# First attention of a two-layer network: TensorE's order of work, the tail's softmax by tile, and the output bias

## The chip, the cores and the metric

The kernel is one launch on one core of one Trainium2 chip. The metric is the device time of the launch in microseconds (us). The kernel before took 3280.93 us in the median of three runs (3278.07 to 3284.38). The engines are TensorE (PE; its weight loads are PEld), VectorE (DVE), ScalarE (ACT), GpSimd (POOL) and SyncE (SP), which issues DMAs. Everything is float32 unless stated.

## The reference, cut to what matters

```python
# x is (8, 512, 256); a layer is half a feed-forward, an attention, half a feed-forward
x = x + 0.5 * L0_ffn(layernorm(x));  x = x + L0_attn(layernorm(x));  x = x + 0.5 * L0_ffn(layernorm(x))
x = x + 0.5 * L1_ffn(layernorm(x));  x = x + L1_attn(layernorm(x));  x = x + 0.5 * L1_ffn(layernorm(x))
# L0_attn: 16 heads of 16, a window of 32 earlier tokens
disp, val = x @ w_disp + b_disp, x @ w_val + b_val
strain = disp_window - disp                              # (B, head, T, 32, 16)
state = mean over the window of (strain @ w_state + b_state)
bond = gelu(strain @ w_strain + b_strain + state @ w_state_i + state_window @ w_state_j + rel_pos @ w_pos)
damage = sigmoid(gelu(strain @ w_damage + b_damage) @ w_damage_out + b_damage_out)
logits = bond @ w_bond_out + b_bond_out - 10 * damage    # masked where the window starts before token 0
out = (softmax(logits) over the window, applied to val_window) @ w_cproj + b_cproj
```

## The kernel before, in words

The network is six phases in a row: feed-forward, first attention, feed-forward, and the same three for the second layer. Only the first attention (`attn0_phase`, L1650 on) is touched. Every engine runs a list of instructions in the order in which it is written and waits on semaphores.

**Chunks and steps.** A batch of 512 tokens is 16 chunks: two halves of eight heads, each with eight groups of four window places. The phase is a loop over steps s (`for s in range(LAST)`, written once for each engine); batch i is s // 16 and the step within it is q = s % 16. There are 128 chunks and 29 steps behind them. For chunk n, DVE makes the bond input in four operations (`bond_chunk`, L2316), POOL the damage input in one (`damage_chunk`, L1984), ACT puts a Gelu over each (L2247, L2252), and TensorE contracts both with a 32-column weight (`columns`, L2031, eight instructions each). Both inputs have rings of three buffers: chunk n is written once TensorE has summed chunk n-3. In step s, DVE and POOL make chunk s+1, ACT handles chunk s, and TensorE sums chunk s-1.

**In the same steps.** Every four chunks ACT makes a tanh (L2260), DVE combines (L2327), TensorE transposes the logits (L2039), and DVE copies them out. At steps 3, 5 and 7 of a batch the softmax of the batch before runs: maximum on DVE (L2350), subtraction on POOL (L1991), exponential on ACT (L2266), sums on DVE (L2355). The softmax rows go to DRAM in 128-byte pieces and come back skewed (`skew_weights`: four stores, L1898, and one load of 2 MB, L1903). Each of the 32 tiles of 128 tokens is then finished in four steps, a new tile every four steps (`finishing`): transposes of the weights (`turn_weights`, L2054), copies by ACT and DVE, 32 small products with the values (`sums`, L2065), division (L2373), transposes (L2092), a copy (L2392), projection with the bias as a one-row product (`project`, L2099, L2100), and addition to x (L2398). A tile's transposes wait for the addition of the tile before.

**Products of a batch.** TensorE makes the terms q, a and c of both halves (`make_q` L2127/L2130, `make_a` L2137/L2140, `make_c` L2147), the values (L2084), the transposed tokens (L2108) and their window means (L2115, L2118), at the steps `A1_Q`, `V_Q`, `XN_Q` and so on. In TensorE's step they all stand ahead of `columns(s - 1)`, which is last. DVE copies each of them out in the same step, behind its own tile work. POOL normalises the tokens of the next batch at step 5 (L1973), and those of batch 0 ahead of the loop.

## Time and profile before

| | |
|---|---|
| median of three runs | 3280.93 us |
| the profiled execution | 3305.36 us |
| its span | 3303.6 us |
| start of the phase to its first chunk on ACT | 670.4 to 720.03 us |
| its 128 chunks | 720.03 to 1364 us |
| its tail, to the last addition | 1364 to 1455.4 us |

The span is cut by the profile's own clock, from the first instruction. The phase begins when the engines leave the barrier at 670.4 us. The row of a stretch gives each engine's busy time; a timeline row gives a start, a length and, in brackets, how long the engine had been idle and who released it. The mean granted TensorE clock of the whole execution was 0.929 of full speed.

### The profile page before, as it was taken

How to read it: one execution, taken by the hardware profiler on the slowest of the kernel's cores; microseconds unless marked ns; L12 is line 12 of the kernel's file. 1: busy time of each engine (PE TensorE's matmuls, PEld its weight loads, DVE VectorE, ACT ScalarE, POOL GpSimd, SP SyncE). 2: the span in 40 equal slices, each digit the busy share in tenths (PEclk: the TensorE clock that was granted, in tenths of full speed). 3: DMA queues.
4: the chain of work that ended last, by engine and by line, in shares of the span. 5: the costliest groups of instructions: out<-in, count | busy, mean ns of one | idle time of the engine just before them, and what ended most of it. 6: DMA issues, size and time to landing. Idle time of an engine off the chain costs nothing. (4 is left out here: it accounts for less than half of the span.)

```text
span 3303.6 us, 53470 instructions
## 1 busy us (share of the span) xinstructions
PE 2872.1 (87%) x19093; PEld 2051.1 (62%) x19093; DVE 1705.9 (52%) x4783; ACT 1560.8 (47%) x2597; POOL 1355.7 (41%) x1339
## 2 busy tenths in 40 slices
PE   3599999958899998645799999799969999998999
PEld 3489899823344443335799999566645666655666
DVE  4711111158787887537311111366676666665666
ACT  1133333329888887512233333233337777782332
POOL 3434444449998898425344444100024434420000
PEclk8699999979999999756899999899989999998999
DMA  7169999820555554942399999400043323401000
GB/s 259 45 216 320 315 315 319 248 64 17 59 60 58 59 59 55 68 150 85 116 324 311 321 307 322 120 1 0 0 111 91 83 68 91 99 14 36 13 13 19
DMA packets 355261, 431.83 MB, mean 131 GB/s; under 512 B 84803, under 2 KB 313046, under 8 KB 350934
## 3 DMA queue, kind: packets, MB, share of 16 engines
q1 hardware_dynamic: 330454, 395.22, 44.5%
q0 software_dynamic: 24576, 33.57, 4.7%
q8 instruction: 140, 2.29, 0.3%
q14 instruction: 91, 0.75, 0.1%
HBM read 355.86 MB, written 72.88 MB: 130 GB/s over the span
## 5 line engine op out<-in xcount | busy, mean ns | idle before, releaser
L1617 ACT ACTIVATE f_h_t<-f_h_ps,f_b_t 128x128 f32<-128x128 f32 x1024 | 320.4, 364 | 621.3 <-PE f_h_ps L1576 621.1
L1984 POOL TENSOR_TENSOR a_dmg_buf<-a_c 128x2048 f32<-128x2048 f32 x128 | 520.1, 4091 | 90.5 <-PE a_dmg_ps L2031 63.4
L1576 PEld LDWEIGHTS f_h_ps<-f_rows_t,f_w 128*128 128x128 f32 x4096 | 482.5, 194 | 9.9 <-issue 3.5
L1576 PE MATMUL f_h_ps<-f_rows_t,f_w 128*128 128x128 f32 x4096 | 483.6, 277 | 2.3 <-DVE f_rows_t L1629 1.2
L1587 PE MATMUL f_y_ps<-f_w,f_h_t 128*128 128x256 f32 x2048 | 462.9, 379 | 0.0
L1536 POOL DMA_INDIRECT acc_rows<-f_y,f_give x128 | 205.1, 1603 | 512.5 <-DMA acc_rows<-f_y,f_give 399.0
L1587 PEld LDWEIGHTS f_y_ps<-f_w,f_h_t 128*128 128x128 f32 x2048 | 379.3, 190 | 46.4
L2316 DVE SCALAR_TENSOR_TENSOR a_bond_buf<-a_a,a_small_rep,a_q_ps 128x512 f32<-128x512 f32 x512 | 347.0, 741 | 41.9 <-PE a_bond_ps L2031 40.2
L428 DVE SCALAR_TENSOR_TENSOR x_resid<-f_y_ps,f_gate,x_resid 128x256 f32 x512 | 218.8, 479 | 162.4 <-PE f_y_ps L311 156.9
L885 ACT ACTIVATE a_prob<-a_prob,a_neg_top 128x384 f32<-128x384 f32 (+3 forms) x512 | 276.5, 570 | 47.8 <-POOL a_neg_top L702 47.5
L299 PE MATMUL f_h_ps<-f_xn_t,f_w 128*128 128x512 f32 x584 | 282.7, 611 | 3.6 <-DMA f_b<-in_L_ffn_bs_dram 1.9
L998 DVE CUSTOM_DVE_ANT_0 a_prob<-a_s_ps,a_factor 128x384 f32<-128x384 f32 (+3 forms) x512 | 234.5, 487 | 86.9 <-PE a_s_ps L779 84.5
L360 ACT ACTIVATE f_h_t<-f_h_ps,f_b 128x512 f32<-128x512 f32 x146 | 100.3, 687 | 368.8 <-PE f_h_ps L299 368.5
L311 PEld LDWEIGHTS f_y_ps<-f_w,f_h_t 128*128 128x128 f32 x1152 | 219.4, 191 | 86.2 <-issue 54.3
L311 PE MATMUL f_y_ps<-f_w,f_h_t 128*128 128x256 f32 x1152 | 270.2, 380 | 0.1
L1629 DVE COPY f_rows_t<-f_t_ps 128x256 f32<-128x256 f32 x128 | 54.4, 425 | 412.9 <-PE f_t_ps L1564 412.9
L2252 ACT ACTIVATE a_dmg_buf<-a_dmg_buf,a_small_rep 128x2048 f32<-128x2048 f32 x128 | 255.2, 1993 | 10.3 <-POOL a_dmg_buf L1984 10.2
L2247 ACT ACTIVATE a_bond_buf<-a_bond_buf,a_bond_act_b 128x2048 f32<-128x2048 f32 x128 | 255.5, 1996 | 8.3 <-DVE a_bond_buf L2316 8.1
L1636 DVE TENSOR_TENSOR f_y_biased<-f_y_ps,f_b 128x256 f32<-128x256 f32 x128 | 54.4, 425 | 393.4 <-PE f_y_ps L1587 378.2
L790 PE MATMUL a_t_ps<-ident,a_prob 128*128 128x128 f32 x1280 | 231.1, 280 | 17.6 <-ACT a_prob_t L896 13.6
L896 ACT COPY a_prob_t<-a_t_ps 128x512 f32<-128x512 f32 (+1 forms) x352 | 192.7, 548 | 100.4 <-PE a_t_ps L790 99.2
L702 POOL TENSOR_SCALAR a_neg_top<-a_top 128x1 f32<-128x1 f32 x512 | 105.7, 210 | 323.5 <-DVE a_top L998 304.0
(322 smaller groups left out, 4326.7 us busy)
## 6 DMA issues: line engine op xcount, KB each, us to landing
f_w<-in_L_ffn_w_dram SPq DMA_DIRECT2D x256, 1024.0 KB
a_skewed<-skew SPq DMA_DIRECT2D x8, 2048.0 KB, 8.5
a_k_s<-parts SPq DMA_DIRECT2D x16, 768.0 KB, 7.8
acc_rows<-x_resid SPq DMA_DIRECT2D x17, 512.0 KB, 4.6
xn_rows<-f_xn SPq DMA_DIRECT2D x16, 512.0 KB, 3.1
x_resid<-acc_rows SPq DMA_DIRECT2D x16, 512.0 KB, 7.6
a_vals<-val_rows SPq DMA_DIRECT2D x64, 128.0 KB, 5.1
skew<-a_bond SPq DMA_DIRECT2D x32, 256.0 KB
```

Of the source, the lines that this page charges most:

```text
L299: last = nc.tensor.matmul(h_ps[(k * NE + n) % 2][:, :], w1_sb[:, RUN[n], c, :], norm.xn_t[k][:, c, :], start=c == 0, stop=c == DC - 1)
L311: last = nc.tensor.matmul(y_ps[m % YB][:, j, :], h[:, t * P:(t + 1) * P], w2_sb[:, RUN[n], :], start=True, stop=True)
L790: last = nc.tensor.transpose(t_ps[pack % TB][:, col + kb * P:col + (kb + 1) * P], prob[:, u % PR, kb * P:(kb + 1) * P], core.ident[:, :])
L885: nc.scalar.activation(prob[:, u % PR, 0:width], prob[:, u % PR, 0:width], ACT.Exp, bias=neg_top[:, u % PR:u % PR + 1]).then_inc(exp_ready, 1)
L998: nc.vector.tensor_tensor_reduce(out=prob[:, u % PR, 0:width], in0=s_ps[use % SB][:, 0:width], in1=factor[:, S - width:S], scale=1.0, scal ...
L1576: last = nc.tensor.matmul(h_ps[n // HB][:, (n % HB) * P:(n % HB + 1) * P], w1_sb[s][:, c, n * P:(n + 1) * P], rows_t[e % 2][:, c, :], star ...
L1587: last = nc.tensor.matmul(y_ps[k][:, 0:D], h_t[k][:, n, :], w2_sb[e % R][:, n, :], start=n == 0, stop=n == HC - 1)
L1617: nc.scalar.activation(h_t[k][:, n, :], h_ps[n // HB][:, (n % HB) * P:(n % HB + 1) * P], ACT.Gelu, bias=b1_t[:, n, e:e + 1]).then_inc(gelu ...
L1984: nc.gpsimd.tensor_tensor(dmg_buf[n % RING][:, :, :], places(c_sb[h], first_place(dg)), c_sb[h][:, PAD:].unsqueeze(1).broadcast_to([P, DG, ...
L2247: nc.scalar.activation(buf[:, :, :], buf[:, :, :], ACT.Gelu, bias=bond_act_b[:, h:h + 1]).then_inc(bond_act, 1)
L2252: nc.scalar.activation(buf[:, :, :], buf[:, :, :], ACT.Gelu, bias=small_rep[:, B_DAMAGE:B_DAMAGE + 1]).then_inc(dmg_act, 1)
L2316: last = nc.vector.scalar_tensor_tensor(out=bond_buf[n % RING][:, dd, :], in0=a_sb[h][:, d + 1:d + 1 + S], scalar=small_rep[:, POS + d:POS ...
```

## The change

- **TensorE's order.** `columns(s - 1)` comes first in a step. The products q and a are cut in halves over two steps (`begin_q`, `end_q`, `begin_a`, `end_a`), and the steps of all products are dealt anew. The values move from steps 3 and 7 to 7 and 15.
- **DVE's copies.** Each product is copied one step later than it is made, right behind `bond_chunk` and ahead of the tile work. `inverse_std(1, B, 2)` stands at the start of step 4, not at its end.
- **Start.** The tokens of batch 0 are normalised by DVE; POOL's `normalise(0)` is gone, and `normalise(i + 1)` stands at step 4.
- **Re-layout by tile.** 16 stores and 4 loads for a batch replace 4 and 1, each tile with semaphores of its own. For the last batch (`soft_parts`), the maximum, subtraction and exponential are also made tile by tile. The softmax of a ninth batch that doesn't exist is no longer run in the tail.
- **Late tiles.** From tile 26 on (`LATE`), a tile begins every two steps and uses PSUM banks that the chunks have left, so that two tiles are in work at a time.
- **Bias.** Three bf16 rows that add up to the float32 bias (`split_bias`, on DVE at step 5) replace the float32 row; the product takes three rows of bf16 ones.

```diff
--- before.py
+++ after.py
...
     FIN = 4
     FIRST = 13
-    LAST = CHUNKS + FIRST + TPB * FIN
+    LATE = FINISHES - TPB - 2
+    LATE_FIN = 2
     NTP = 8
     XN, XM, A0, C0, A1, C1 = 0, 2, 4, 5, 6, 7
-    V_Q = (3, 7)
-    XN_Q, XM_Q, Q0_Q, A0_Q, C0_Q = 7, 9, 11, 12, 13
-    A1_Q, C1_Q, Q1_Q = 1, 2, 3
+    A1_Q, C1_Q, Q1_Q = 0, 3, 4
+    V_Q = (7, 15)
+    XN_Q, XM_Q, A0_Q, C0_Q, Q0_Q = 6, 8, 10, 12, 13
...
+        b_out_rows = sb("b_out_rows", [3, D], BF16)
+        ones = sb("ones", [3, P], BF16)
...
+        second = lambda m: dmg_ps if m >= LATE else o_ps
+        ctx_bank = lambda m: bond_ps[1][:, 0:D] if m >= LATE else o_ps[:, D:2 * D]
+        project_bank = lambda m: bond_ps[0] if m >= LATE else o_ps
...
+        def begin(m):
+            return FIRST + (m + TPB) * FIN if m <= LATE else begin(LATE) + (m - LATE) * LATE_FIN
+        FINISH_AT = {begin(m): m for m in range(FINISHES)}
+        LAST = begin(FINISHES - 1) + FIN
         def finishing(s, stage):
-            x, now = divmod(s - FIRST, FIN)
-            return x - TPB if s >= FIRST and now == stage else None
+            return FINISH_AT.get(s - stage)
...
-            return i - 1 if now == q and i > 0 else None
+            return i - 1 if now == q and 0 < i <= B else None
...
+        def soft_parts(j):
+            return [slice(x, x + 1) for x in range(TPB)] if j == B - 1 else [slice(0, TPB)]
...
             def skew_weights(j):
-                sp.wait_ge(exp_done, j + 1)
-                if j:
-                    sp.wait_ge(skew_loaded, j * 16)
-                for a in range(BPT):
-                    row = TPB * NH * SPAN
-                    rows = bass.AP(tensor=skew_dram.tensor, offset=a * WIN * row + 1,
-                                   ap=[[row + 1, WIN], [SPAN, TPB * NH], [1, WIN]])
-                    sp.dma_start(rows, bond[j % 2][a * WIN:(a + 1) * WIN, :, :, :].rearrange(
-                        "p j h w -> p (j h) w")).then_inc(skew_stored, 16)
-                if j:
-                    sp.wait_ge(w_turned, j * TPB)
-                sp.wait_ge(skew_stored, (j + 1) * 16 * BPT)
-                sp.dma_start(skewed[:, :, :].rearrange("p j s -> p (j s)"), skew_dram).then_inc(skew_loaded, 16)
+                row = TPB * NH * SPAN
+                for x in range(TPB):
+                    if x < len(soft_parts(j)):
+                        sp.wait_ge(exp_done, j + x + 1)
+                    if j:
+                        sp.wait_ge(skew_loaded[x], j * 16)
+                    for a in range(BPT):
+                        rows = bass.AP(tensor=skew_dram.tensor, offset=a * WIN * row + x * NH * SPAN + 1,
+                                       ap=[[row + 1, WIN], [SPAN, NH], [1, WIN]])
+                        sp.dma_start(rows, bond[j % 2][a * WIN:(a + 1) * WIN, x, :, :]).then_inc(skew_stored[x], 16)
+                for x in range(TPB):
+                    if j:
+                        sp.wait_ge(w_turned, (j - 1) * TPB + x + 1)
+                    sp.wait_ge(skew_stored[x], (j + 1) * 16 * BPT)
+                    sp.dma_start(skewed[:, x, :], skew_dram[:, x * NH * SPAN:(x + 1) * NH * SPAN]
+                                 ).then_inc(skew_loaded[x], 16)
...
-            normalise(0)
+                for n, tiles in enumerate(soft_parts(j)):
+                    count = tiles.stop - tiles.start
+                    rows = bond[j % 2][:, tiles, :, :].rearrange("p j h w -> p (j h) w")
+                    pool.wait_ge(top_ready, j + n + 1)
+                    nc.gpsimd.tensor_tensor(rows, rows, top[:, tiles.start * NH:tiles.stop * NH, :].broadcast_to([P, count * NH, WIN]),
+                                            ALU.subtract).then_inc(soft_ready, 1)
...
             for k in range(NX):
...
-                if q == 5 and i + 1 < B:
+                if q == 4 and i + 1 < B:
...
             def turn_weights(m):
                 j, x = divmod(m, TPB)
-                if x == 0:
-                    pe.wait_ge(skew_loaded, (j + 1) * 16)
-                before = values_before(FIRST + (m + TPB) * FIN)
+                pe.wait_ge(skew_loaded[x], (j + 1) * 16)
...
-                if m:
+                if m > LATE:
+                    pe.wait_ge(w_copied_act, m)
+                    pe.wait_ge(w_copied_dve, m)
+                elif m == LATE:
+                    pe.wait_ge(tanh_done, ALL_GROUPS)
+                elif m:
                     pe.wait_ge(proj_added, m)
...
-                    bank = (t_ps, o_ps)[hp // 4]
+                    bank = (t_ps, second(m))[hp // 4]
...
                 pe.wait_ge(w_copied_act, m + 1)
...
+                if m == LATE:
+                    pe.wait_ge(proj_added, m)
+                if m > LATE:
+                    pe.wait_ge(ctx_ready, m)
...
             def turn_ctx(m):
                 pe.wait_ge(ctx_ready, m + 1)
+                if m == LATE:
+                    pe.wait_ge(logits_copied, ALL_GROUPS)
+                if m > LATE:
+                    pe.wait_ge(ctx_copied, m)
...
                 pe.wait_ge(ctx_copied, m + 1)
+                if m == 0:
+                    pe.wait_ge(b_out_split, 1)
+                if m > LATE:
+                    pe.wait_ge(proj_added, m)
                 for c in range(DC):
-                    nc.tensor.matmul(o_ps[:, 0:D], ctx_t[:, c, :], w_out_sb[:, c, :], start=c == 0, stop=False)
-                nc.tensor.matmul(o_ps[:, 0:D], ones[:, :], b_out_sb[:, :], start=False, stop=True).then_inc(proj_ready, 1)
+                    nc.tensor.matmul(project_bank(m)[:, 0:D], ctx_t[:, c, :], w_out_sb[:, c, :], start=c == 0, stop=False)
+                nc.tensor.matmul(project_bank(m)[:, 0:D], ones[:, :], b_out_rows[:, :], start=False, stop=True).then_inc(proj_ready, 1)
...
+            def begin_q(i, h):
                 if i:
...
+            def end_q(i, h):
                 for c in range(DC):
...
-            def make_a(i, h):
+            def begin_a(i, h):
...
+            def end_a(i, h):
                 for c in range(DC):
...
             for s in range(LAST):
                 i, q = divmod(s, STEPS)
+                if 0 < s <= CHUNKS:
+                    columns(s - 1, 0)
+                    columns(s - 1, 1)
...
+                if i < B:
+                    if q == A1_Q:
+                        begin_a(i, 1)
+                    if q == A1_Q + 1:
+                        end_a(i, 1)
+                    if q == C1_Q:
+                        make_c(i, 1)
+                    if q == Q1_Q:
+                        begin_q(i, 1)
+                    if q == Q1_Q + 1:
+                        end_q(i, 1)
                 if i + 1 < B:
...
-                    if q == Q0_Q:
-                        make_q(i + 1, 0)
...
+                        begin_a(i + 1, 0)
+                    if q == A0_Q + 1:
+                        end_a(i + 1, 0)
...
-                if 0 < s <= CHUNKS:
-                    columns(s - 1, 0)
-                    columns(s - 1, 1)
+                    if q == Q0_Q:
+                        begin_q(i + 1, 0)
+                    if q == Q0_Q + 1:
+                        end_q(i + 1, 0)
+                if i < B and q in V_Q:
+                    values(s, i, V_Q.index(q))
...
+                for n, tiles in enumerate(soft_parts(j)):
+                    act.wait_ge(soft_ready, j + n + 1)
+                    nc.scalar.activation(bond[j % 2][:, tiles, :, :], bond[j % 2][:, tiles, :, :], ACT.Exp).then_inc(exp_done, 1)
...
+                for tiles in soft_parts(j):
+                    nc.vector.tensor_reduce(top[:, tiles.start * NH:tiles.stop * NH, 0],
+                                            bond[j % 2][:, tiles, :, :].rearrange("p j h w -> p (j h) w"),
+                                            AX.X, ALU.max).then_inc(top_ready, 1)
...
@@ -2389,13 +2452,30 @@
...
+            def split_bias():
+                dve.wait_ge(loaded, LOADED)
+                nc.vector.tensor_copy(b_out_part[:, 0, :], b_out_sb[:, :])
+                nc.vector.drain()
+                nc.vector.tensor_tensor(b_out_rest[:, :], b_out_sb[:, :], b_out_part[:, 0, :], ALU.subtract)
...
+                nc.vector.scalar_tensor_tensor(out=b_out_rows[:, :], in0=b_out_rest[:, :], scalar=core.ident[0:3, 2:3],
+                                               in1=b_out_sum[:, :], op0=ALU.mult, op1=ALU.add).then_inc(b_out_split, 1)
...
-            inverse_std(0, 1, 1)
+            dve.wait_ge(std_ready, 1)
+            nc.vector.reciprocal(rstd[:, 0:TPB], std[:, 0:TPB])
+            nc.vector.drain()
+            for j in range(TPB):
+                last = nc.vector.tensor_scalar(xn[:, j, :], core.tile(1, j), mean_var[:, j, 0:1], rstd[:, j:j + 1],
+                                               ALU.subtract, ALU.mult)
+            last.then_inc(xn_ready, 1)
...
             for s in range(LAST):
-                i, q = divmod(s, STEPS)
+                if s == 4:
+                    inverse_std(1, B, 2)
                 if s + 1 < CHUNKS:
                     bond_chunk(s + 1)
+                i, q = divmod(s - 1, STEPS)
+                if 0 < s and i < B:
+                    if q == A1_Q + 1:
...
+                    if q in V_Q:
+                        copy_values(i, V_Q.index(q))
                 m = finishing(s, 0)
                 if is_tile(m):
...
-                if i < B and q in V_Q:
-                    copy_values(i, V_Q.index(q))
...
-                if s == 4:
-                    inverse_std(1, B, 2)
+                if s == 5:
+                    split_bias()
...
```

## Rows read from the trace of the kernel before

**Rows 1.** Stretches: start:end, length, busy us (instructions) of five engines, TensorE clock, DMA share, GB/s.
```profile
720.03:792.37 72.34, 59.76 (x344) 20.90 (x344) 65.63 (x143) 65.89 (x39) 68.91 (x21) 0.91 0.05 15
792.37:869.56 77.19, 63.31 (x430) 25.26 (x430) 58.82 (x89) 69.09 (x42) 71.81 (x22) 0.96 0.57 59
...
952.24:1034.09 81.85, 74.86 (x685) 33.66 (x685) 66.67 (x106) 69.86 (x45) 73.51 (x22) 0.96 0.53 59
1286.76:1364.00 77.24, 62.06 (x624) 25.97 (x623) 58.74 (x93) 68.52 (x44) 64.88 (x17) 0.91 0.58 62
...
```

**Rows 2.** Timeline of batch 3, its steps 3 and 4: start us, length, engine, line.
```profile
967.82 1.88 PE L2127 MATMUL a_q_ps<-a_xn_t,a_token_w 128*128 128x512 f32 x4
971.34 1.07 PE L2031 MATMUL a_bond_ps<-a_bond_buf,a_col_bond 128*32 128x512 f32 x8
973.20 1.13 PE L2099 MATMUL a_o_ps<-a_w_out,a_ctx_t 128*128 128x256 f32 x4
976.87 0.69 ACT L2260 ACTIVATE a_tanh<-a_dmg_ps,a_damage_b 128x512 f32<-128x512 f32 x1 [4.52 <-PE a_dmg_ps L2031]
```

**Rows 3.** Timeline of the same batch, at its step 12.
```profile
1021.66 0.69 ACT L2260 ACTIVATE a_tanh<-a_dmg_ps,a_damage_b 128x512 f32<-128x512 f32 x1 [6.35 <-PE a_dmg_ps L2031]
1021.70 3.72 POOL L1984 TENSOR_TENSOR a_dmg_buf<-a_c 128x2048 f32<-128x2048 f32 x1 [3.41 <-PE a_dmg_ps L2031]
```

**Rows 4.** Groups by line in batch 3: count, busy us, mean ns, idle before.
```profile
L2100 PE MATMUL a_o_ps<-a_b_out,a_ones 1*128 1x256 f32 x9 | 3.3, 432 | 0.0
L2355 DVE TENSOR_REDUCE a_inv_sum<-a_bond 128x64 f32<-128x2048 f32 x1 | 2.3, 2277 | 0.0
L2266 ACT ACTIVATE a_bond<-a_bond 128x2048 f32<-128x2048 f32 x1 | 1.9, 1909 | 0.0
L2266 ACT ACT_TABLE_LOAD x1 | 1.3, 1283 | 0.0
```

**Rows 5.** One line over the whole trace: bf16 products of the feed-forward, min/median/max ns.
```profile
L1308 PE MATMUL f_pos_ps<-f_mask,f_before x16: 272/273/421, 38.9 to 1591.9; 128*128 128x256 bf16 x16
```

**Rows 6.** Timeline of the start of the phase.
```profile
679.87 5.00 POOL L1973 TENSOR_SCALAR a_xn<-x_resid,a_mean_var,a_rstd 128x256 f32<-128x256 f32 x4
680.96 0.49 DVE L2452 TENSOR_TENSOR a_inner<-a_diag,a_small_rep 128x128 f32<-128x128 f32 x2
684.93 1.11 PE L2108 MATMUL a_tok_ps<-ident,a_xn 128*128 128x128 f32 x4 [4.75 <-POOL a_xn L1973]
```

**Rows 7.** SyncE's issues in the timeline of batch 3: the re-layout's stores and load.
```profile
984.59 10.62 SPq L1898 DMA_DIRECT2D skew<-a_bond  x4
1009.89 0.34 SPq L1903 DMA_DIRECT2D a_skewed<-skew  x1
```

**Rows 8.** The stores' line over the whole trace, ns of one issue: min/median/max.
```profile
L1898 SPq DMA_DIRECT2D skew<-a_bond x32: 318/2384/8584, 822.6 to 1387.1; - x32
```

**Rows 9.** Timeline near the end of batch 7, its step 13.
```profile
1354.13 1.12 PE L2054 MATMUL a_t_ps<-ident,a_skewed 128*128 128x128 f32 x4 [5.69 <-DMA a_skewed<-skew]
```

**Rows 10.** Timeline of the tail: softmax of the last batch, its re-layout, its four tiles.
```profile
1373.51 2.29 DVE L2350 TENSOR_REDUCE a_top<-a_bond 128x64 f32<-128x2048 f32 x1
1375.87 3.64 POOL L1991 TENSOR_TENSOR a_bond<-a_bond,a_top 128x2048 f32<-128x2048 f32 x1 [12.39 <-DVE a_top L2350]
1381.48 12.57 SPq L1898 DMA_DIRECT2D skew<-a_bond  x4
1415.87 1.11 PE L2054 MATMUL a_t_ps<-ident,a_skewed 128*128 128x128 f32 x4 [18.17 <-DMA a_skewed<-skew]
1432.92 1.22 PE L2100 MATMUL a_o_ps<-a_b_out,a_ones 1*128 1x256 f32 x2
1446.10 1.08 PE L2054 MATMUL a_t_ps<-ident,a_skewed 128*128 128x128 f32 x4 [0.61 <-DVE x_resid L2398]
1454.95 0.42 DVE L2398 TENSOR_TENSOR x_resid<-a_o_ps,x_resid 128x256 f32<-128x256 f32 x1 [3.31 <-PE a_o_ps L2100]
```

**Rows 11.** The stretch of the last four tiles, in the columns of rows 1.
```profile
1415.80:1456.00 40.20, 27.75 (x320) 18.00 (x320) 12.90 (x19) 4.14 (x5) 3.64 (x1) 0.50 0.02 4
```

91 lines of the change are left out of this document (43 added, 48 removed).

## The prediction

> **What bounds the kernel now.** I read the stretches first, cut at ACT's first Gelu of each batch [rows 1]. A batch of the first attention takes 72.3 us (batch 0), 77.2 (batch 1), then more: batches 2 to 6 lie between 869.56 and 1286.76, 83.4 us each, with batch 3 (81.9) as the example. In batch 3 no engine is full: TensorE 74.9, POOL 73.5, ACT 69.9, DVE 66.7. So no engine's rate sets the 82 us; waits between four nearly full engines do. The reader should see in that row that the floor of a batch is about 73.5 to 75 and that some 8 us are lost.
>
> The timeline says where. At step 3 TensorE makes q from 967.82 to 971.34 (3.5 us, eight matmuls at 1.88 for four) before it sums the chunk that ACT had ready; the sum then takes 1.86 (971.34 to 973.20), and ACT stands still for 4.5 us until TensorE's sums let it go on [rows 2]. At step 12 it is the same with q at step 11 and a at step 12 in a row: ACT idle 6.35, POOL 3.4 [rows 3]. These two places are 10.9 us of ACT's time, about what its idle share shows (81.85 - 69.86 = 12.0). The release is TensorE's sum each time: a ring buffer comes free only after products that nobody needs yet.
>
> A third place stays: the exponential. It holds ACT for a table load, 1.9 us of work and a table load back, 4.5 us [rows 4].
>
> In the tail one chain runs with nothing beside it [rows 10]: maximum at 1373.51, stores at 1381.48, the load landed at 1415.87 (TensorE idle 18.2), then four tiles in a row to 1455.37. At the start, TensorE waits 4.75 us for POOL's normalised tokens [rows 6].
>
> **The start.** POOL begins to normalise at 679.87, late, and takes 5.0. DVE makes two operations of 128x128 in 0.49, so four of 128x256 take at most 2 us, and it made the statistics itself, before its wait for the small weights. TensorE can then go on at once; the next thing it needs is DVE's diagonal matrices, ready at 681.45 (680.96 + 0.49), where it now begins its token transposes at 684.93 and ends them at about 685.8. Everything after that is a chain of TensorE and DVE, which moves up: -4 us. Bounds: 0 (if a weight load is late instead) to -4.75, the wait itself. POOL's memsets move up too, so they take no cover away. The one-step move of `normalise(i + 1)` puts its 4 x 1.25 us right behind the softmax subtraction of 3.6 on POOL; both fall where ACT is held 4.5 by the exponential, and tokens are needed only two steps later. I take 0, bounds 0 to +2 a batch, inside the range of the batch below.
>
> **The batches.** `columns` first takes the 3.5 us of q and a out of the way of the ring. What is late next? TensorE's own work: 74.9 busy in batch 3, less what the bias saves. That float32 row costs two instructions of 0.43 for a tile, the start-to-start distance being about that; four tiles give about 3.3 us a batch [rows 4]. One bf16 instruction of 256 columns is 0.27 [rows 5], so 4 x 0.27 = 1.1 stays; with overlap of pipelined ends I count -2 of the -2.2. TensorE needs 72.9 then, POOL 73.5, ACT 69.9: POOL is the floor. Above it I put two waits. First, the exponential: ACT gives no chunk for 4.5 us and then a copy, while TensorE has only 4 us of other work. Second, at step 7 DVE's sum of 2.3 [rows 4] with its reciprocal stands behind the token copy; the next copy, which TensorE's window means of step 8 wait for, comes up to 2.8 late. Together 7.3 at most; the ring of three chunks covers about half. I take +3.5: 77 us a batch; bounds 73.5 (the ring covers all) and 81 (nothing covered).
>
> The halves cost nothing by themselves: the same matmuls, and `tok_ps` is held for one step more, which the new steps leave room for. The later copies mean that DVE finds its product ready and waits less for TensorE; TensorE finds the bank free one step later, in which it has no other product for it. q of the next batch's first half now ends at step 14, one step ahead of the chunk that reads it, instead of three. That chunk starts up to 3 us later on DVE, against a ring slack of about one step: 0, bounds 0 to +2, in the same range. The values arrive at DRAM nine steps later than before, but their tile starts 13 steps into the next batch: 0. `split_bias` is seven operations on three partitions at step 5 of batch 0: 0.25 each as in [rows 6], 1.8 us, and I count +1. The earlier `inverse_std` waits for a square root that is done by then: 0.
>
> So, from [rows 1]: batch 0 72.3 to 71, batch 1 (no tiles until step 13) 77.2 to 74.5, batches 2 to 6 from 417.2 to 385, batch 7 from 77.2 to 71.5, since ACT's 68.5 is its floor and the wait of 5.7 for the re-layout [rows 9] goes. That wait goes because the first tile no longer needs the whole 2 MB. From the first store to the load's issue 25.3 us pass [rows 7], from the first store to the landed load 34.4 (1381.48 to 1415.87), so the load is about 9 and its first quarter 2.3: the first tile has its weights some 6 us sooner. Sum of the batches: 644.0 to 602, -42. Bounds: 73.5 and 81 for batches 2 to 6 (367.5 and 405) and 1.5 either way for each other batch give 580 and 626.5, so -64 to -17.5.
>
> **The tail.** The first tile's exponential is ready after a quarter each of 2.29, 3.64 and 1.91: 2.0 us after 1373.51, so its stores go out at about 1375.6, 5.9 earlier than 1381.48 [rows 4, 10]. All stores together are the same 8192 pieces, so I leave them 25.3 us, and the first load queues behind them: 1375.6 + 25.3 + 2.3 = 1403, against 1415.87: -12.5. Bounds: -6 (loads no faster for being cut) and -20 (the first load passes the stores).
> Then the tiles. TensorE is busy 27.75 us for four, at half clock (0.50) [rows 11], 6.9 a tile; the float32 bias row is 1.22 of it [rows 10] and becomes one bf16 product, 0.42 at this clock [rows 5]: 6.1. Two tiles in work hide the waits for copies except some 0.2, so a tile every 6.3 us. The last still runs its whole chain: 1446.10 to 1455.37 is 9.3, less 0.8. 3 x 6.3 + 8.5 = 27.4 instead of 39.5, in which the superfluous ninth softmax also had a part: -12. Tail together -24.5; bounds -14 to -32.
>
> The row of the stretch shows 0.50, the lower level of 1.2 GHz, after TensorE had stood idle for 18 us [rows 10, 11]. The Trainium skill (TensorE: Matmul & The Clock Gate, "What's actually happening") says that the throttled clock is the default and that activity releases it, so tiles packed closer could bring the 2.4 GHz back; by that rule the tail would be some 10 us shorter still. The trace has it at 0.50 for the whole stretch, though busy for 69% of it.
>
> **Sum.** -4 - 42 - 24.5 = -70.5, made against the profiled execution (3305.4, span 3303.6): 3235. It lies 24.4 above the median of the runs, so 3281 - 70.5 = 3210.5.
>
> **Rivals.**
> *POOL's floor.* All waits vanish and the batches run at 73.5: -4 - 64 - 24.5, 3188.5. For it: in batch 3 POOL waited for nothing but TensorE's sums where I looked, as at step 12. Against: the exponential's 4.5 and the coupling of four engines at over 90%.
> *The waits only move.* TensorE needs nearly the whole of every step now, so the chunk is never early, and DVE, which copies products before it combines logits, hands its delay to ACT's tanh. The batches keep 82, and only the start, the wait of batch 7 and the tail pay: -4 - 6 - 24.5, 3246.5. For it: TensorE 74.9 of 81.9 busy. Against: the two stalls sit exactly behind q and a.
> *The clock comes back in the tail.* 272 and 421 ns for one product are the two levels in this trace [rows 5]. At the upper one the tile period falls from 6.3 to about 3.9 and the last chain by 2.5: -10 more, 3200.
> *Slower: the issue of the stores.* Four stores hold SyncE 10.6 to 12.6 us [rows 7, 10]. If a store costs its 3.1 whatever its size, sixteen take 50 and the first load goes out 25 us later. In batch 3 it landed at about 1018.9 (1009.89 + 9), and TensorE was ready for the tile behind the sums that released 1021.66 [rows 3]: 2.8 to spare. So seven batches lose 22 each, 154, the tail 25 - 6 - 12 = 7, and the start gives 4: 3438. It decides from the point where sixteen issues take more than about 28 us. Against: the shortest issue of this line is 318 ns [rows 8], so 3.1 is a full queue and not a price for one.
>
> **Chances.** Forecast 0.57, POOL's floor 0.13, waits only move 0.17, clock 0.09, issue 0.04. Range: from 3188, just past POOL's floor, to 3246. Faster by over 0.2% (6.6 us, about what separates a change from none here) 0.94, within it 0.02, slower 0.04.
>
> **What would show it.** In the profile after: ACT's idle time on TensorE's damage sums at steps 3 and 12 falls from 4.5 and 6.35 to under 1; batches 2 to 6 at 75 to 79; the first chunk 4 us sooner after the barrier; stores of the tail 2 us after the maximum; the first tile at about 30 us after it; tiles every 6.3; one bias product of 0.27. It is wrong if a batch stays above 81 (the order was not the cause), if ACT waits for DVE's bond input in place of TensorE, or if TensorE still waits for the skewed load in the batches.

## The result, and the profile after

The kernel after takes 3264.84 us (3257.48 to 3268.97), the kernel before beside it 3279.26 (3271.79 to 3286.40): ratio 0.9947, interval 0.9935 to 0.9959. It is faster by 14.4 us where 70.5 were forecast, outside the range. Its profiled execution took 3265.07, span 3263.3, clock 0.935. Of all executions told of below one, of the kernel e9, took 4910.35 us at a granted clock of 0.553, and it is left out of e9's median.

The columns of the next rows are those of [rows 1]: batch 0, batch 1, batches 2 to 6 together, batch 3.

```profile
714.95:801.66 86.71, 59.55 (x337) 21.63 (x338) 80.72 (x146) 65.54 (x39) 69.33 (x21) 0.84 0.00 1
801.66:874.19 72.53, 65.31 (x439) 23.70 (x438) 60.59 (x92) 68.55 (x41) 72.53 (x22) 0.93 0.60 66
874.19:1278.35 404.16, 370.74 (x3402) 161.42 (x3401) 331.41 (x526) 351.99 (x216) 369.84 (x107) 0.96 0.50 60
954.39:1035.01 80.62, 74.14 (x682) 32.38 (x681) 66.30 (x106) 70.38 (x43) 73.50 (x22) 0.96 0.52 60
```

Batch 0 is 14 us longer than in [rows 1], with DVE busy 80.7 and not 65.6. Batches 2 to 6 take 80.8 each, not 77. TensorE is busy 74.1 of them, not 72.9.

**Batch 0.** Timeline at step 5: the split of the bias on DVE (3x256 each), then POOL and ACT beside it.

```profile
744.78 2.45 DVE L2466 CAST a_b_out_part<-a_b_out 3x256 bf16<-3x256 f32 x1
747.30 4.16 DVE L2468 TENSOR_TENSOR a_b_out_rest<-a_b_out,a_b_out_part 3x256 f32<-3x256 f32 x1
751.39 4.60 DVE L2469 TENSOR_SCALAR a_b_out_sum<-a_b_out_part,ident 3x256 f32<-3x256 bf16 x1
756.06 3.75 DVE L2471 CAST a_b_out_part<-a_b_out_rest 3x256 bf16<-3x256 f32 x1
759.88 0.41 DVE L2473 TENSOR_TENSOR a_b_out_rest<-a_b_out_rest,a_b_out_part 3x256 f32<-3x256 f32 x1
...
743.37 16.29 POOL L2011 TENSOR_TENSOR a_dmg_buf<-a_c 128x2048 f32<-128x2048 f32 x4
...
763.91 2.00 ACT L2306 ACTIVATE a_bond_buf<-a_bond_buf,a_bond_act_b 128x2048 f32<-128x2048 f32 x1 [12.84 <-DVE a_bond_buf L2376]
```

Four operations of three rows take 15 us, and the last of them ends at 759.81, where POOL's four damage inputs end (743.37 + 16.29 = 759.66). The fifth takes 0.41. The next bond input is behind them, and ACT waits 12.84 for it.

A second small operation of DVE is late in the same batch, at step 3:

```profile
733.39 2.18 DVE L2513 TENSOR_SCALAR a_std<-a_mean_var 128x28 f32<-128x28 f32 x1
```

It ends at 735.57, and POOL's damage inputs at 735.53. In the kernel before it takes 0.18 with POOL idle. Step 3 of batch 0 goes from 10.3 to 12.3 us with it, and the step with the split from 3.8 to 16.7; steps 2 and 12 give back 2.1.

**The start.** DVE and POOL again.

```profile
678.26 2.78 DVE L2543 COPY a_b_state<-a_small_rep 128x2 f32<-128x2 f32 x1
678.33 2.72 DVE L2482 COPY a_xn_t<-a_tok_ps 128x512 f32<-128x512 f32 x1
...
677.51 3.50 POOL L2029 MEMSET a_vals<- 128x4096 f32 x1
```

A copy of two columns and the copy of the tokens behind it end with POOL's memset (681.0). The same copy takes 0.69 elsewhere.

**Batch 3.** Timeline of its steps 3 to 6, where [rows 2] had ACT idle for 4.52; then two groups of the waits of 870 to 1260 (total us, times, longest).

```profile
972.62 2.29 DVE L2412 TENSOR_REDUCE a_top<-a_bond 128x64 f32<-128x2048 f32 x1
974.99 3.64 POOL L2020 TENSOR_TENSOR a_bond<-a_bond,a_top 128x2048 f32<-128x2048 f32 x1 [3.46 <-DVE a_top L2412]
977.57 2.00 ACT L2306 ACTIVATE a_bond_buf<-a_bond_buf,a_bond_act_b 128x2048 f32<-128x2048 f32 x1 [0.87 <-DVE a_bond_buf L2376]
982.38 2.00 ACT L2311 ACTIVATE a_dmg_buf<-a_dmg_buf,a_small_rep 128x2048 f32<-128x2048 f32 x1 [2.80 <-POOL a_dmg_buf L2011]
988.13 0.76 PE L2100 MATMUL a_o_ps<-a_vals,a_turned 128*32 128x32 f32 x64 [2.04 <-ACT a_turned L2332]
991.45 1.94 PE L2059 MATMUL a_bond_ps<-a_bond_buf,a_col_bond 128*32 128x512 f32 x8 [1.97 <-ACT a_bond_buf L2306]
```

```profile
ACT a_bond_buf L2306 <- DVE a_bond_buf L2376: 20.2, 19, 2.4
ACT a_dmg_buf L2311 <- POOL a_dmg_buf L2011: 16.5, 10, 2.8
```

ACT no longer waits for TensorE at steps 3 and 12. Instead POOL stands 3.46 us for the maximum, its next damage input is late behind the subtraction, and ACT waits 2.80 for that. At other steps ACT waits for DVE's bond input, 19 times, about 1 us each. This is what the prediction named as a sign against itself.

**The tail.** The lines that answer to [rows 10], and the stretch that answers to [rows 11].

```profile
1362.49 2.46 DVE L2412 TENSOR_REDUCE a_top<-a_bond 128x16 f32<-128x512 f32 x4
1364.99 17.92 SPq L1925 DMA_DIRECT2D skew<-a_bond  x16
1383.01 8.64 SPq L1930 DMA_DIRECT2D a_skewed<-skew  x4
1391.99 1.12 PE L2085 MATMUL a_t_ps<-ident,a_skewed 128*128 128x128 f32 x4 [16.87 <-DMA a_skewed<-skew]
1397.11 0.66 PE L2085 MATMUL a_t_ps<-ident,a_skewed 128*128 128x128 f32 x4
1400.99 0.66 PE L2085 MATMUL a_t_ps<-ident,a_skewed 128*128 128x128 f32 x4
1404.87 0.66 PE L2085 MATMUL a_t_ps<-ident,a_skewed 128*128 128x128 f32 x4
1408.54 0.28 PE L2143 MATMUL a_bond_ps<-a_b_out_rows,a_ones 3*128 3x256 bf16 x1
1411.08 0.42 DVE L2461 TENSOR_TENSOR x_resid<-a_bond_ps,x_resid 128x256 f32<-128x256 f32 x1 [1.43 <-PE a_bond_ps L2143]
```

```profile
1391.90:1411.50 19.60, 16.30 (x323) 12.30 (x323) 8.27 (x18) 2.34 (x4) 0.00 (x0) 0.90 0.27 84
```

The first tile starts 29.5 us after the maximum (forecast 30). The second tile follows after 5.1 us, the next two every 3.9, because the granted clock is 0.90 here and not 0.50: the transposes go from 1.12 to 0.66.

### The profile page after: what moved, and what is told of

Its sections match the earlier page's. It is cut to its first block and busy times, and to the rows that moved or that the text cites. A ratio compares the mean times of both kernels' runs of the same rounds, so it can differ in the third digit from the quotient of the medians.

```text
span 3263.3 us, 53594 instructions
## 1 busy us (share of the span) xinstructions
PE 2850.5 (87%) x19061; PEld 2036.4 (62%) x19061; DVE 1717.9 (53%) x4794; ACT 1559.6 (48%) x2599; POOL 1346.0 (41%) x1337
## 5 line engine op out<-in xcount | busy, mean ns | idle before, releaser
L1636 DVE TENSOR_TENSOR f_y_biased<-f_y_ps,f_b 128x256 f32<-128x256 f32 x128 | 54.3, 425 | 393.4 <-PE f_y_ps L1587 384.3
```

## The experiments

Two measures are used beside the medians. A batch is the distance between ACT's bond Gelus sixteen apart. A step is the distance between two neighbours, as a mean over batches 2 to 6. "Phase" is from DVE's first statistics to those of the next phase. "Start" ends at the first bond Gelu, "tail" begins with the end of the last damage Gelu. The ratio is that to the kernel before, run beside each, with its 95% interval; before stood at 3279.3 to 3282.8 in the median. All columns but the first are from one profiled execution of each kernel. The rest of the span is code that no run touches, and it took 2513.0 to 2524.2 us in these executions, so a few us between two medians need not come from the edit. The profiled execution of e9 took 3267.71 us, 13.9 above its median, that of e11 3259.24, 6.7 above, that of e13 3225.75, 3.9 below.

| kernel | median us (ratio, interval) | start | batch 0 | batches 2 to 6, each | tail | phase |
|---|---|---|---|---|---|---|
| before, as in the rows | 3280.93 | 49.6 | 72.3 | 83.4 | 91.3 | 786.4 |
| e1 before, once more | 3279.40 (0.9994, 0.9982 to 1.0005) | 49.6 | 72.3 | 81.5 | 85.7 | 763.0 |
| after | 3264.84 (0.9947, 0.9935 to 0.9959) | 47.8 | 86.7 | 80.8 | 59.1 | 745.9 |
| e2 bias split early | 3253.84 (0.9915, 0.9902 to 0.9928) | 43.8 | 71.6 | 80.5 | 63.1 | 729.3 |
| e3 old order | 3251.45 (0.9903, 0.9889 to 0.9917) | 47.5 | 76.1 | 81.1 | 58.7 | 734.9 |
| e4 bias alone | 3268.55 (0.9956, 0.9944 to 0.9969) | 47.4 | 73.2 | 80.0 | 83.2 | 750.4 |
| e5 subtraction late | 3234.52 (0.9855, 0.9837 to 0.9872) | 44.4 | 71.8 | 78.0 | 61.9 | 714.2 |
| e6 no exponential | 3247.18 (0.9887, 0.9870 to 0.9903) | 44.2 | 71.4 | 80.8 | 61.4 | 726.4 |
| e7 less TensorE | 3240.07 (0.9866, 0.9849 to 0.9882) | 45.5 | 73.1 | 79.0 | 61.5 | 723.4 |
| e8 less POOL | 3251.63 (0.9900, 0.9882 to 0.9918) | 47.6 | 72.1 | 80.6 | 60.5 | 731.2 |
| e9 e5, old order | 3253.79 (0.9918, 0.9900 to 0.9935) | 47.3 | 76.1 | 82.4 | 58.6 | 741.8 |
| e10 e5, small memsets | 3235.36 (0.9863, 0.9844 to 0.9882) | 47.9 | 72.2 | 78.1 | 61.4 | 717.3 |
| e11 normalise at 5 | 3252.55 (0.9917, 0.9900 to 0.9935) | 47.0 | 73.8 | 81.0 | 61.6 | 737.2 |
| e12 e10, no exponential | 3226.48 (0.9837, 0.9819 to 0.9854) | 47.5 | 72.1 | 77.0 | 60.7 | 707.0 |
| e13 e5, tile ahead | 3229.66 (0.9847, 0.9830 to 0.9864) | 48.1 | 72.2 | 76.8 | 60.9 | 711.0 |
| e14 e5, whole products | 3241.65 (0.9877, 0.9858 to 0.9896) | 44.0 | 72.9 | 79.5 | 62.2 | 723.1 |
| e15 e5, less TensorE | 3221.87 (0.9817, 0.9801 to 0.9833) | 44.7 | 73.1 | 76.2 | 61.3 | 705.1 |

Steps of a batch, us, start to start of the bond Gelus (the four others are 2, 8, 10 and 14):

| step | 0 | 1 | 3 | 4 | 5 | 6 | 7 | 9 | 11 | 12 | 13 | 15 | the four others | batch |
|---|---|---|---|---|---|---|---|---|---|---|---|---|---|---|
| e1 before | 4.4 | 4.3 | 4.0 | 9.1 | 8.9 | 3.8 | 3.8 | 4.3 | 3.9 | 10.9 | 4.3 | 3.8 | 16.2 | 81.5 |
| after | 4.4 | 5.2 | 4.4 | 5.3 | 11.8 | 3.8 | 3.8 | 5.4 | 5.4 | 4.5 | 5.2 | 5.2 | 16.4 | 80.8 |
| e5 | 4.4 | 5.2 | 4.5 | 5.3 | 8.9 | 3.8 | 3.8 | 5.7 | 5.2 | 4.4 | 5.3 | 5.2 | 16.3 | 78.0 |
| e9 | 4.4 | 4.3 | 3.8 | 8.3 | 8.9 | 3.8 | 5.5 | 4.3 | 4.2 | 10.6 | 4.3 | 3.8 | 16.5 | 82.4 |
| e12 | 4.4 | 5.2 | 4.5 | 5.3 | 6.1 | 5.8 | 4.0 | 5.1 | 5.2 | 4.4 | 5.2 | 5.2 | 16.5 | 77.0 |
| e13 | 4.8 | 4.3 | 4.4 | 5.3 | 8.9 | 4.1 | 4.1 | 4.3 | 5.0 | 5.6 | 4.3 | 5.4 | 16.5 | 76.8 |

**e1: the kernel before, unchanged.**

> The kernel before, unchanged. The change moved its median by -14, but the two profiles differ by -40, all of it inside the first attention. Theory A (the profile that the prediction was made against was one slow execution): this profile is some 20 to 26 us shorter than 3303.6, and the gap is found inside the first attention, in stalls that the first profile has and this one lacks. Theory B (the profiler costs the kernel before more than the kernel after): this profile is again near 3304 while the timed runs are near 3279.

Its profiled execution took 3279.34, near the median, and its phase 763.0 where that of the rows took 786.4. Nearly the whole difference between the two executions (26.0) lies in the phase that the prediction was about (23.4): batch 1 3.6, batches 2 to 6 9.6, batch 7 4.6, the tail 5.6. One such place, in the timeline of the first execution, is a wait of TensorE for nothing that the profile shows:

```profile
1257.85 1.94 PE L2031 MATMUL a_dmg_ps<-a_dmg_buf,a_col_damage 128*32 128x512 f32 x8 [4.52 <-issue]
```

**e2: the bias split ahead of the loop.**

```diff
             nc.vector.drain().then_inc(biases_ready, 1)
+            split_bias()
-                if s == 5:
-                    split_bias()
```

> The kernel after with one edit: the seven DVE operations that split the bias stand ahead of the loop, where DVE waits 9 us for TensorE and GpSimd is idle, not at step 5. Theory A (at step 5 each of them waits for GpSimd's 4 us damage operation to end, since the two engines exclude each other on such operands): they take 0.2 to 0.5 us each here, batch 0 falls from 86.7 to 72 us and the kernel from 3265 to about 3250. Theory B (they are slow for what they are, three partitions or the casts): they take 2.5 to 4.6 us each here too, the start of the phase gets 8 us longer, and the kernel gains at most 6 us.

Its split in the timeline (first three of seven):

```profile
698.59 0.28 DVE L2466 CAST a_b_out_part<-a_b_out 3x256 bf16<-3x256 f32 x1 [0.47 <-issue]
698.95 0.41 DVE L2468 TENSOR_TENSOR a_b_out_rest<-a_b_out,a_b_out_part 3x256 f32<-3x256 f32 x1
699.29 0.34 DVE L2469 TENSOR_SCALAR a_b_out_sum<-a_b_out_part,ident 3x256 f32<-3x256 bf16 x1
```

With POOL idle they take 0.28, 0.41 and 0.34. Batch 0 falls from 86.7 to 71.6, the phase by 16.6, the median by 11.0. Theory A holds.

**e11: the kernel after, with POOL's normalising back at step 5.**

```diff
-                if q == 4 and i + 1 < B:
+                if q == 5 and i + 1 < B:
                     normalise(i + 1)
```

> The kernel after with one change: POOL's normalise of the next batch back at step 5, beside which DVE splits the bias. Theory A (the seven small operations of the split are held by the damage inputs that POOL makes beside them, an operation with two SBUF inputs; beside the normalising, which has one, they pass): the split takes 2.5 to 4 us and not 16, batch 0 falls from 86.7 to 73 to 75, the median to 3250 to 3255. Rival B (the new place of the split in DVE's order, behind the copies of products, is what costs): batch 0 stays at 85 to 87, the median 3262 to 3268. Batches 2 to 6 as after, 80 to 81.

Split and normalising in its timeline:

```profile
745.95 0.32 DVE L2466 CAST a_b_out_part<-a_b_out 3x256 bf16<-3x256 f32 x1
746.34 0.62 DVE L2468 TENSOR_TENSOR a_b_out_rest<-a_b_out,a_b_out_part 3x256 f32<-3x256 f32 x1
746.89 0.33 DVE L2469 TENSOR_SCALAR a_b_out_sum<-a_b_out_part,ident 3x256 f32<-3x256 bf16 x1
747.30 0.32 DVE L2471 CAST a_b_out_part<-a_b_out_rest 3x256 bf16<-3x256 f32 x1
...
746.11 5.00 POOL L2000 TENSOR_SCALAR a_xn<-x_resid,a_mean_var,a_rstd 128x256 f32<-128x256 f32 x4
```

Same place in DVE's order, another operation beside it: 0.3 to 0.7 each, batch 0 at 73.8, the median 12.3 lower. Theory A holds. So the one-step move of the normalising, which the prediction costed at 0 to +2, put the damage inputs beside the split, and that was 12.9 of batch 0's 14.4 us. The Trainium skill (SBUF — State Buffer, "Who interferes with whom") says that copies, casts and tensor_scalar operations of DVE can take a port pair that it shares with GpSimd, and that whichever of the two issues second then blocks fully. It says of a DVE operation with two SBUF inputs that it contends with a GpSimd operation that reads SBUF. The trace agrees beside the damage inputs (up to 4.60 in place of 0.34). Beside POOL's tensor_scalar, which reads SBUF as well (1.25 us each), it shows no such block: the seven operations take at most 0.26 more than with POOL idle.

**e3 and e9: the old order of TensorE and DVE**, in e3 on top of e2 and in e9 on top of e5. DVE's copies go back to their old places too, and so do `inverse_std` and POOL's `normalise(i + 1)` (step 5). In the new order the place of the normalising changes nothing in batches 2 to 6 (81.0 in e11, 80.8 in the kernel after).

```diff
-    A1_Q, C1_Q, Q1_Q = 0, 3, 4
-    V_Q = (7, 15)
-    XN_Q, XM_Q, A0_Q, C0_Q, Q0_Q = 6, 8, 10, 12, 13
+    V_Q = (3, 7)
+    XN_Q, XM_Q, Q0_Q, A0_Q, C0_Q = 7, 9, 11, 12, 13
+    A1_Q, C1_Q, Q1_Q = 1, 2, 3
...
-                if 0 < s <= CHUNKS:
-                    columns(s - 1, 0)
-                    columns(s - 1, 1)
...
+                if 0 < s <= CHUNKS:
+                    columns(s - 1, 0)
+                    columns(s - 1, 1)
```

> As the kernel with the early split, but TensorE's order, its steps, and DVE's copies are those of before (columns last, products whole, copies in the same step). Start, tail and bias stay changed. Theory A (the new order is worth the 3 us a batch that the two profiles show): batches 2 to 6 take 83, and the kernel is 15 to 22 us slower than with the early split. Theory B (the bf16 bias and the re-layout by tile gave what the batches gained, the order nothing): within 5 us of it.

> e5 with the order of TensorE and DVE put back to that of the kernel before (the sums last in a step, products whole, copies in the same step); the subtraction stays at step 4, the bias is split ahead of the loop. Theory A (the order is worth nothing, since TensorE was full at the old stalls; what counted was POOL standing for the maximum): batches 2 to 6 at 78 to 79 as in e5 (78.0), the median within 6 us of e5's 3234.5. Rival B (the order pays once the wait at step 5 is gone, because only then is TensorE's place the next limit): batches at 80 or more, the median 3246 or above. Theory A's own condition: e3 against e2 gave +0.5 us a batch the other way round, so a difference of 0 to 1 us a batch fits it.

e3 against e2: nothing to choose (3251.5 and 3253.8). I took that as "the order is worth nothing", and e9 refutes it. With the subtraction late, the old order is 19.3 us slower in the median (3253.8 against 3234.5), and 4.4 us a batch in the profiled executions. The 4.4 is likely too high, by how much is not known: e9's profile lies 13.9 above its median, and its phase is 27.5 longer than e5's where the medians are 19.3 apart. The table of steps shows why both are true. The new order takes 10.3 us a batch from steps 4 and 12 (9.1 and 10.9 in e1, 5.3 and 4.4 in e5). In the kernel after it pays 2.9 of this back at step 5. The old order has 8.9 there with the subtraction early (e1) and late (e9), so moving it gives nothing there: POOL's wait lay beside ACT's old stall at step 4. Batch 0 takes 76.1 in both, mostly because the small operation of step 3 is held longer still (3.08 us, from 734.22 to 737.30 in e3, where POOL's damage input ends at 737.27) and that step takes 13.2. Two of ACT's waits in e9's batch 3, the old stalls come back:

```profile
971.10 0.69 ACT L2314 ACTIVATE a_tanh<-a_dmg_ps,a_damage_b 128x512 f32<-128x512 f32 x1 [3.80 <-PE a_dmg_ps L2059]
1016.96 0.69 ACT L2314 ACTIVATE a_tanh<-a_dmg_ps,a_damage_b 128x512 f32<-128x512 f32 x1 [5.58 <-PE a_dmg_ps L2059]
```

**e4: the kernel before with the bf16 bias alone**, split at step 5.

```diff
+                if s == 5:
+                    split_bias()
...
-                nc.tensor.matmul(o_ps[:, 0:D], ones[:, :], b_out_sb[:, :], start=False, stop=True).then_inc(proj_ready, 1)
+                nc.tensor.matmul(o_ps[:, 0:D], ones[:, :], b_out_rows[:, :], start=False, stop=True).then_inc(proj_ready, 1)
```

> The kernel before with the bias change alone: bf16 rows, and their split at DVE's step 5 as in the change. Theory A (the split costs 14 to 15 us in batch 0, the product saves 0.4 us of TensorE a tile): batch 0 is 14 us longer than before, batches 2 to 6 are 1 to 2 us shorter, the tail 3 shorter, and the kernel is 0 to 8 us slower than before. Theory B (the cost in batch 0 comes from the new order): batch 0 stays at 72 and the kernel is 8 to 12 us faster.

The split stands at step 5 here as well, but beside POOL's normalising, as in e11, and takes 3.0 us: batch 0 is 73.2. So theory A fails, and of B the time holds (12.8 us faster): the cost in batch 0 is not in the split alone but comes with the new places. The bias product gives 1.5 us a batch and 2.5 in the tail. Its ratio is 0.9956 where the whole change has 0.9947: this part alone has most of the gain as it stood, since batch 0 took back about half of what the tail gave.

**e5: POOL's subtraction one step later.**

```diff
-                j = softmax_batch(s, 3)
+                j = softmax_batch(s, 4)
                 if j is not None:
                     less_top(j)
```

> As the kernel with the early split, with one edit: GpSimd subtracts the softmax maximum at step 4, behind the damage input of chunk 5, and not at step 3 ahead of it, where it waits 3.5 us for the maximum and makes ScalarE wait 2.8 us for chunk 5. Theory A (TensorE bounds a batch: 74 us of work and 6.6 idle around the exponential; the idle 1.7 us that this stall puts on TensorE goes): batches 2 to 6 fall from 80.5 to 78.5 or 79, the kernel by 9 to 14 us. Theory B (GpSimd's 8.5 us in a row then delay the next damage input as much): batches stay at 80.5 and the kernel within 3 us of 3254.

19.3 us less than e2 in the median, 15.1 in the phase. Step 5 falls from 11.8 to 8.9, and no other step moves by more than 0.3.

**e6 and e12: the exponential replaced by a copy**, on e2 and on e10.

```diff
-                    nc.scalar.activation(bond[j % 2][:, tiles, :, :], bond[j % 2][:, tiles, :, :], ACT.Exp).then_inc(exp_done, 1)
+                    nc.scalar.copy(bond[j % 2][:, tiles, :, :], bond[j % 2][:, tiles, :, :]).then_inc(exp_done, 1)
```

> As the kernel with the early split, but ScalarE's exponential of the first attention is a plain copy of the same size, so the two table loads around it go (2.6 us); the weights are then the shifted logits. Theory A (TensorE bounds a batch and stands idle only where the exponential holds ScalarE; its clock falls there too, so that the next chunk's sums take 1.9 instead of 1.1): batches 2 to 6 fall by 2.6 to 4.5, to 76 to 78. Theory B (GpSimd or VectorE sets the 80.5): within 1 us of 80.5.

> e10 with ACT's exponential replaced by a copy of the same size, so that no table is loaded for it; the rows are not exponentiated. What is left above POOL's 73.5 in e5 is 4.5 us a batch, and the longest step is the one with the exponential, 8.9 us against some 4.9 for a step. Theory A (ACT's 4.5 us for it are what holds the batch now that POOL no longer stands there): batches 2 to 6 at 75 to 76, the median 3218 to 3224. Rival B (the loss is spread over the four engines' coupling and moves, as in e6, where it gained 0): batches 77 to 78, 3230 to 3235.

In e6 step 5 falls to 9.0 and step 6 grows to 6.2. The mean is 80.8, as in e2, but one batch of the five took 83.6; the other four have 80.1 and the median is 6.7 lower, so that a gain of under 1 us a batch can't be excluded. In e12 it gives 1.2 a batch and 8.9 in the median. Neither theory has it whole. ACT is held 2.6 us less, but the steps behind take back more than half of it.

**e7 and e8: less of TensorE, less of POOL**, on e2. e7's edit (the first two; `end_a` likewise) and e8's.

```diff
             def end_q(i, h):
-                for c in range(DC):
+                for c in range(DC - 1, DC):
...
-                for j in range(TPB):
+                for j in range(TPB - 1, TPB):
```

> As the kernel with the early split, but each of the four mean products of a batch (halves end_q, end_a) takes one of its two input halves only, which leaves out 4 x 0.86 = 3.4 us of TensorE's work a batch. Theory A (TensorE is the bound of a batch): batches 2 to 6 fall by 2.5 to 3.4, to 77 to 78. Theory B (GpSimd with 73.5 busy and its waits is the bound): they fall by under 1 us.

> As the kernel with the early split, but GpSimd normalises only one of the four token tiles of each later batch, which leaves out 3.6 us of its work a batch at step 4. Theory A (TensorE is the bound): batches 2 to 6 stay within 0.7 us of 80.5. Theory B (GpSimd is the bound): they fall by 2.5 to 3.6.

TensorE's 3.4 us less gave 1.5 a batch; POOL's 3.6 less gave nothing in the batches (80.6) and 2.2 in the median, which the intervals don't separate from e2. So POOL's busy time doesn't set the length of a batch in e2. No run takes work from POOL in e5, where it no longer stands for the maximum.

**e10: POOL's long memset in sixteen.**

```diff
-            nc.gpsimd.memset(vals[:, :, :, :], 0.0).then_inc(pads_ready, 1)
+            for n in range(NBLK):
+                last = nc.gpsimd.memset(vals[:, n, :, :], 0.0)
+            last.then_inc(pads_ready, 1)
```

> e5 with POOL's one memset of the values' rows (3.50 us) cut into 16. Theory: the long memset holds DVE's copy of the first transposed tokens (2.72 us in the kernel after, 0.69 elsewhere), and with short ones DVE gets in between: the copy at 0.7 to 1.1 us, the start of the phase 1 to 2 us shorter than e5's 44.4, the median 3232 to 3234. Rival: sixteen memsets cost POOL more than they give (its issue for each), POOL's first damage input comes later and the start is as long or up to 2 us longer: 3234 to 3237. Batches as in e5, 78.0.

The copy and the memsets in its timeline:

```profile
683.50 2.36 DVE L2484 COPY a_xn_t<-a_tok_ps 128x512 f32<-128x512 f32 x1
...
681.73 4.10 POOL L2030 MEMSET a_vals<- 128x256 f32 x16
```

My theory failed. The copy still ends where the last memset does (685.86 and 685.83), and the 128x2 copy ahead of it takes 2.43. The length of one memset isn't what counts; DVE's copies didn't get in between sixteen. Its tensor_tensor operations of 128x128 were not held: three of them take 0.69 from 682.31 on, beside the memsets, as much as in the kernel before. The start is longer than e5's for another reason, below.

**e13, e14, e15: what gives back the other 6.4 us**, each on top of e5. e13 puts TensorE's work for a tile ahead of the sum, e14 makes q and a whole in one step, e15 has the edit of e7. The diffs of e13 and e14 (for q of the second half, the three others likewise):

```diff
+                m = finishing(s, 0)
+                if is_tile(m):
+                    turn_weights(m)
...
+                    project(m)
                 if 0 < s <= CHUNKS:
                     columns(s - 1, 0)
                     columns(s - 1, 1)
```

```diff
                     if q == Q1_Q:
                         begin_q(i, 1)
-                    if q == Q1_Q + 1:
                         end_q(i, 1)
```

> e5 with TensorE's work for a tile (transposes of the weights, sums, transposes, projection) ahead of the sum of the chunk, as before; the products stay behind it, in halves. Theory A (ACT and DVE now wait for the tile's work behind the sum, and hand that on to the bond input): the steps that grew, 1, 3, 9, 11, 13, 15, fall by 0.5 to 1 us each, batches 2 to 6 at 74.5 to 76.5, the median 3214 to 3225. Rival B (TensorE has no gap there, so its order within a step changes nothing): batches 77.5 to 78.5, the median 3231 to 3238.

> e5 with q and a made whole in one step (the step in which the first half stood). Theory A (the halves spread TensorE's load so that no step is over the pace): whole products put 3.8 us more into single steps, batches 2 to 6 at 79 to 81, the median 3242 to 3252. Rival B (the ring evens it out, the halves are worth nothing, or cost): 77.5 to 78.5, within 5 us of e5's 3234.5.

> e5 with the second half of q and a cut from two matmul groups to one, 3.4 us less of TensorE's time a batch; the window means' second half is left out of q and a. In e5 TensorE is busy 74.1 us of 78.0. Theory A (TensorE's total is what holds the grown steps): batches 2 to 6 at 75 to 76, the median 3215 to 3222, with POOL at 73.4 the next floor. Rival B (waits between engines, not TensorE's total): batches at 77 or more, the median above 3228.

Batches 2 to 6 of e1, e5 and e13, in the columns of [rows 1]:

```profile
863.79:1271.36 407.57, 373.45 (x3421) 168.17 (x3420) 332.79 (x526) 349.45 (x217) 367.20 (x106) 0.96 0.48 59
```

```profile
857.88:1248.11 390.23, 370.42 (x3402) 162.92 (x3401) 331.63 (x526) 351.46 (x216) 369.19 (x107) 0.97 0.53 62
```

```profile
859.20:1243.13 383.93, 356.34 (x3402) 162.17 (x3401) 331.38 (x526) 351.98 (x216) 368.81 (x107) 1.00 0.51 63
```

e13: steps 1, 9 and 13, where a tile's transposes stand behind the sum, fall by 1.0, 1.4 and 1.0; step 12 takes 1.2 back. It gains 1.2 a batch, 3.2 in the phase and 4.9 in the median, less than theory A had, and the intervals of e13 and e5 overlap: the gain isn't clear of the noise. Its granted clock is 1.00, and TensorE's busy time falls by 14.1 over five batches with the same 3402 matmuls. e14: the halves are worth 1.5 a batch (7.1 in the median), so theory A holds. e15: 3.1 us less of TensorE a batch gives 1.9, and 12.7 in the median, near theory A. It comes from steps 1, 3, 13 and 15 (0.4 each, 0.5 at 15); steps 9 and 11 fall by under 0.2. So TensorE's time is shown to be part of what e5's steps grew by, and its order behind the sum is likely another part. Together they don't cover the 6.4, and nothing here splits the rest. Of the kernels that leave nothing out e13 is the fastest: 3229.7, ratio 0.9847.

## Why the prediction was wrong, step by step

**The base, 24.3 of the 54.3 us between 3210.5 and 3264.8.** The working gave 3235 for a profiled execution, measured 3265. Then 24.4 were taken off, the first execution's excess over the median. But 23.4 of that excess lay in the first attention itself (e1), and the gains were counted on the same stretches: the median has neither the 83.4 of a batch, nor the whole 5.7 of [rows 9], nor the tail's 91.3. The excess was used twice. The forecast lengths add up to a phase of 715.9 (45.6 + 603.5 + 66.8, to the last damage Gelu); with e1's 763.0 as the base that is -47.1, or 3232, and not 3210.5.

The remaining 30, term by term, new lengths as forecast against the kernel after:

| term | forecast | measured | off |
|---|---|---|---|
| start | 45.6 | 47.8 | +2.2 |
| batch 0 | 71 | 86.7 | +15.7 |
| batch 1 | 74.5 | 72.5 | -2.0 |
| batches 2 to 6 | 385 | 404.2 | +19.2 |
| batch 7 (to the last damage Gelu) | 73.0 | 75.5 | +2.5 |
| tail | 66.8 | 59.1 | -7.7 |

**"`split_bias` ... 1.8 us, and I count +1."** Failed: the seven take 16 us, and their step gets 12.9 longer. The price was taken from a row in which POOL makes a tensor_scalar beside DVE [rows 6], and what POOL makes beside the split after the change was not worked through. e2, e4 and e11 settle it. Another 2.0 of batch 0 are the small operation of step 3, held in the same way by its times; no run takes that one apart.

**"I take +3.5: 77 us a batch; bounds 73.5 and 81."** The value failed, the bounds held. That the stalls at steps 3 and 12 sit behind q and a was right: steps 4 and 12 of the table fall by 3.8 and 6.4, near the 10.9 that the prediction read there. What failed is what is late next. The prediction named the exponential and DVE's sum at step 7. Step 7 didn't move at all (3.8). What came was POOL's wait for the maximum, 2.9 at step 5 (e5), and 0.9 to 1.5 us in each of the steps 1, 9, 11, 13 and 15, with the 0.4 of step 3 6.4 in all, of which e13 and e15 explain a part. The maximum stands behind a copy of products and tile work on DVE, and POOL issues the subtraction ahead of the next damage input. The prediction didn't ask what is queued behind POOL's wait for it, which ACT's old stall had covered.

**"TensorE needs 72.9."** 74.1. Of the 2 us of the bias, e4 has 1.5 in the batch's length and 1.9 in busy time (364.20 against 373.45 over five batches); the kernel after has 1.3 more than e4 again, at a clock of 0.96 against 0.97, and e13, at full clock, has 71.3.

**"POOL is the floor."** Not what held the batches: less of POOL's work changed nothing (e8). A busy time near the length doesn't set it where that engine waits for another in between. As a lower bound the 73.5 was not tested; the shortest batch in the table is 76.2 (e15).

**The rival "the waits only move"** (3246.5) was nearest in kind for the batches. It failed as an explanation that the order can't pay: it pays once the subtraction is moved (e9 against e5, 19.3 us in the median).

**The start, -4.** Measured -1.8, with a granted clock of 0.70 in either; e2, with 0.77, has 43.8, and e4, with the old start and 0.74, 47.4. DVE's normalising does its part, and 2.0 of it go to the copy held by the memset. The prediction said that POOL's memsets "take no cover away"; they moved up onto DVE's copy.

**Batch 7.** The wait of 5.69 is gone, as forecast. But it is 2.10 in e1, which has the batch at 74.2 without any change, 4.6 less than the first execution (78.8). The kernel after has 75.5, so nothing was won.

**The tail.** Forecast -24.5, measured -26.6 against e1 (85.7 to 59.1). The re-layout is as worked out. The tiles came at 3.9 and not 6.3, because the clock rival was true: 0.09 was too low for it. The granted clock of the last four tiles is 0.50 where the tail is the old one (e1, e4) and 0.85 to 0.90 where it is the new one (the kernel after, e3, e5, e13), each time after TensorE had stood idle for 14 to 20 us. In e2, e5 and others the tail takes 61 to 63. The Trainium skill (TensorE: Matmul & The Clock Gate, "What's actually happening") says that activity releases the throttled clock. The trace agrees, with 0.90 against 0.50. The prediction put that rival's tail 10 us below its forecast; it came out 7.7 below.

**Slower: the issue of the stores.** Refuted: sixteen issues take 17.92 together where four took 12.57 [rows 10].

**What stays open.** Why TensorE's clock is 1.00 in e13's batches and 0.97 in e5's, and how much of e13's 4.9 us is that clock and how much the order, was not separated. Nor is it known what holds the rest of the 6.4 us in e5's steps, or how far POOL's busy time bounds a batch there.

## What to carry to other kernels

Before a gain is counted on a stall, see that it is in more than one execution: where a profile is slower than the median, find where the excess lies, and don't take it off twice. Where an instruction is moved, read what runs on the other engine in that slot afterwards, its operands too; a few rows by 256 columns can cost as much as the largest operation beside it. When a stall is removed, list what had been waiting in its shadow: moving POOL's subtraction by one step took the gain from 27.5 us (e2) to 48.2 (e5), and gave nothing in the old order (e9), so an order can be judged only with its neighbours set for it.
